# The second norm's scale and bias moved from the weights to ScalarE's copy out of PSUM

## The reference, cut to what matters

```python
def layer_norm(x, w, b, eps=1e-05):
    mu = jnp.mean(x, axis=-1, keepdims=True)
    var = jnp.mean(jnp.square(x - mu), axis=-1, keepdims=True)
    return (x - mu) * lax.rsqrt(var + eps) * w + b
...
# a feed-forward layer: attention on layer_norm(x, ln1_w, ln1_b) is added, then
def moe_ff(x, w_gate, w1, b1, w2, b2):       # x is layer_norm(., ln2_w, ln2_b)
    probs = jax.nn.softmax(t @ w_gate, axis=-1)
    tw, ti = lax.top_k(probs, TOP_K)          # 2 of 8 experts
    tw = tw / jnp.sum(tw, axis=-1, keepdims=True)
    for e in range(N_EXPERTS):
        we = jnp.sum(jnp.where(ti == e, tw, 0.0), axis=-1)
        h = jax.nn.gelu(t @ w1[e] + b1[e]) @ w2[e] + b2[e]
        out = out + we[:, None] * h
```

## Time and profile before

| | us |
|---|---|
| median of 3 runs | 1042.02 (1041.05 to 1045.36) |
| profiled execution | 1043.29 |
| its span, from the first to the last instruction | 1041.3 |
| busy TensorE / VectorE / ScalarE / GpSimd | 991.2 / 558.0 / 604.9 / 395.4 |
| mean granted TensorE clock | 0.959 of full speed |

### The profile page before, as it was taken

The page is one execution under the profiler, slowest core; times in us unless marked ns, Lnnn a source line. Parts: engine busy times, 40 slices in busy tenths (PEclk is TensorE's granted clock), DMA queues, the critical chain, the costliest instruction groups (busy, mean ns, idle before and its releaser), DMA issues.

```text
span 1041.3 us, 22226 instructions
## 1 busy us (share of the span) xinstructions
PE 991.2 (95%) x8516; PEld 745.7 (72%) x8516; DVE 558.0 (54%) x1427; ACT 604.9 (58%) x1128; POOL 395.4 (38%) x839
## 2 busy tenths in 40 slices
PE   3999999999999999999999999899999999999998
PEld 2655555666655999999886555566665699999997
DVE  4877777788884212122336788678888322111111
ACT  1356666887887454444445777688777744444443
POOL 6858676757743100012022353736873310000000
PEclk9677888999999999999999999899999999999999
DMA  8000000000000000000000000000000000000000
GB/s 286 2 2 2 3 2 2 3 3 3 3 3 2 1 1 1 2 1 1 1 2 1 3 3 2 3 3 3 3 2 3 2 2 4 8 1 11 1 11 11
DMA packets 9960, 10.42 MB, mean 10 GB/s; under 512 B 1528, under 2 KB 7552, under 8 KB 9856
## 3 DMA queue, kind: packets, MB, share of 16 engines
q1 hardware_dynamic: 8848, 7.64, 2.3%
q10 hardware_dynamic: 1008, 1.38, 0.4%
HBM read 7.44 MB, written 1.05 MB: 8 GB/s over the span
## 4 chain that ended last, share of the span: by engine, by line
PE 79%; DVE 15%; POOL 3%; issue 3%; ACT 0%; DMA 0%; DVEq 0%; ACTq 0%; POOLq 0%
PE bankR L625 22%; PE bankO L387 11%; PE bankE L406 8%; DVE M L986 7%; PE bankE L360 6%; PE bankE L614 6%; PE bankE L616 6%; PE bankE L615 6%; PE bankE L397 2%; DVE QKV L948 2%; PE bankR L373 2%; PE bankR L457 1%; PE bankR L427 1%; PE bankR L475 1%; PE bankE L467 1%
## 5 line engine op out<-in xcount | busy, mean ns | idle before, releaser
L986 DVE TENSOR_REDUCE M<-bankR 128x2 f32<-128x512 f32 x512 | 326.6, 684 | 97.2 <-PE bankR L373 95.9
L741 ACT ACTIVATE Pr<-bankE 128x512 f32<-128x512 f32 x512 | 277.5, 595 | 132.7 <-PE bankE L360 128.9
L845 ACT ACTIVATE Pr<-bankE,b1c 128x512 f32<-128x512 f32 x256 | 171.8, 689 | 176.1 <-PE bankE L616 175.0
L1141 DVE SCALAR_TENSOR_TENSOR X<-bankR,WE,X 128x128 f32<-128x128 f32 x256 | 72.1, 344 | 332.7 <-PE bankR L625 332.7
L625 PEld LDWEIGHTS bankR<-w,Pr 128*128 128x128 f32 x2048 | 238.3, 192 | 6.3 <-issue 1.1
L625 PE MATMUL bankR<-w,Pr 128*128 128x128 f32 x2048 | 238.8, 275 | 0.9 <-DVE X L1141 0.9
L373 PE MATMUL bankR<-KQ 32*128 32x256 f32 x1024 | 170.1, 346 | 6.6 <-DVE M L986 4.5
L387 PE MATMUL bankO<-Pr,Vx 128*32 128x256 f32 x2048 | 173.0, 413 | 0.6 <-ACT OT L733 0.5
L360 PEld LDWEIGHTS bankE<-KQ 32*128 32x128 f32 x1024 | 81.8, 194 | 101.5 <-issue 64.3
L360 PE MATMUL bankE<-KQ 32*128 32x256 f32 x1024 | 136.1, 343 | 0.0
L373 PEld LDWEIGHTS bankR<-KQ 32*128 32x128 f32 x1024 | 108.8, 197 | 16.2 <-DVE M L986 11.7
(11 more groups left out here) (166 smaller groups left out, 1185.7 us busy)
## 6 DMA issues: line engine op xcount, KB each, us to landing
THL<-in_w SPq DMA_DIRECT2D x1, 2048.0 KB, 8.9
KQ<-MT SPq DMA_DIRECT2D x128, 4.0 KB
X<-in_x SPq DMA_DIRECT2D x8, 128.0 KB, 6.6
out_x<-X SPq DMA_DIRECT2D x4, 256.0 KB, 2.3
ropeA<-in_ropeA ACTq DMA_DIRECT2D x1, 384.0 KB, 5.2
ropeB<-in_ropeB ACTq DMA_DIRECT2D x1, 384.0 KB, 5.5
w_lo_rope<-in_w_qkv_rope ACTq DMA_DIRECT2D x1, 192.0 KB, 2.9
b_qkv_rope<-in_b_qkv_rope ACTq DMA_DIRECT2D x1, 192.0 KB, 4.3
```

Of the source, the lines that this page charges most:

```text
L741: nc.scalar.activation(Pr[:, (h // HG) % 2, h % HG], act_bank("S", layer, b, h).rearrange("p (k q) -> p k q", k=TT), ACT.Exp, scale=EXP_SC ...
L845: nc.scalar.activation(G[:, e % 2, c, :], act_bank("hid", ph, at, c), ACT.Gelu_apprx_tanh, bias=b1c[:, e * FC + c:e * FC + c + 1]).then_in ...
L986: v.tensor_reduce(M[:, b % 2, :, h], dve_bank("raw", layer, b, h).rearrange("p (t k) -> p t k", t=TT), AX.X, ALU.max, negate=True).then_in ...
L1141: v.scalar_tensor_tensor(xt[:, j, t, :], dve_bank("out", ph, at)[:, t * D:t * D + D], WE[:, j * BT + t, e:e + 1], xt[:, j, t, :], ALU.mult ...
```

## The change

The second norm's scale and bias are laid on u itself. GpSimd's `close` leaves u in fp32 and does not split it. TensorE turns it by two fp32 transposes into half a bank. ScalarE's `do_uT` is two instructions: one activation (Identity) with the scale and the bias as columns of `lncols`, PSUM to the new tile UT in fp32, and a copy that rounds UT to THL's first half. VectorE's new `rest_of_u` takes the rest to THL's second half. The folding of scale and bias into w1, b1 and w_gate is gone on all engines; the one for b_qkv, which belongs to the first norm, stays in step m = (0, 0). TensorE's gate matmuls stand behind raw scores 5 in place of raw scores 4. VectorE's gate copy and `choose` stand behind maxima 5, `weigh` stands at the end of the step, and ScalarE's exponential for the gate behind its last exponentials. `early` also holds in the step in which p is block (3, 0). Tables of counts (`NFOLD`, `u_ready`, `uT_copied`) and the unused tiles follow.

The core of the diff:

```diff
             def do_uT(layer, b):
                 if LAYERS[layer] == "ffn":
-                    need(pe, u_ready, layer, b, 8)
+                    need(pe, u_ready, layer, b, 6)
                     ring_e.take(pe, ("uT", layer, b))
-                    for x in range(2):
-                        for t in range(TT):
-                            k = turn_r(act_bank("uT", layer, b), 2 * x + t, Uhl[:, x, t, :])
+                    for t in range(TT):
+                        k = turn(act_bank("uT", layer, b)[:, t * P:t * P + P], U[:, t, :], ident[:])
                     k.then_inc(uT.sem, 1)
-                    ring_e.give(("uT", layer, b), uT_copied, layer, b)
+                    ring_e.give(("uT", layer, b), uT_copied, layer, b, 1)
 
             def do_gate(layer, b):
                 if LAYERS[layer] == "ffn":
-                    need(pe, uT_copied, layer, b)
+                    need(pe, u_rest, layer, b)
                     ring_r.take(pe, ("gate", layer, b))
...
                     ring_r.give(("gate", layer, b), gate_copied, layer, b)
 
-            def do_fold(e):
-
-
-                if e == 0:
-                    pe.wait_ge(in_ffn, 8 * 16)
-                    pe.wait_ge(ready_pool, 7)
-                ring_r.take(pe, ("fold", e))
-                bank = dve_bank("fold", e)
-                if e == 0:
-                    mm(bank[:, 0:3 * D], lnb1[:], w_qkv["ffn"][:], start=True, stop=True)
-                    mm(bank[:, 384:384 + E], lnb2[:], w_gate[:], start=True, stop=True)
-                for c in range(FC):
-                    k = mm(bank[:, 400 + c:401 + c], w1raw[:, e, c * P:c * P + P], lnb2[:, 0:1], start=True, stop=True)
-                k.then_inc(fold, 1)
-                ring_r.give(("fold", e), folded, 0, 0, NFOLD - E + e + 1)
+            def do_fold():
+
+                pe.wait_ge(in_ffn, 8 * 16)
+                pe.wait_ge(ready_pool, 6)
+                ring_r.take(pe, ("fold",))
+                mm(dve_bank("fold")[:, 0:3 * D], lnb1[:], w_qkv["ffn"][:], start=True, stop=True).then_inc(fold, 1)
+                ring_r.give(("fold",), folded, 0, 0)
 
...
                 if t:
                     do_outT(*t)
-                if m and m[0] == 0:
-                    do_fold(m[1])
+                if m == (0, 0):
+                    do_fold()
                 if a:
...
                 if m:
                     do_raw(*m, 4)
+                if n and LAYERS[n[0]] != "rope":
+                    do_kT(*n)
+                if a:
+                    do_pv(*a, 1, 1)
+
+                if m:
+                    do_mT(*m, 0)
+                if a:
+                    do_scores(*a, 6)
+                if m:
+                    do_raw(*m, 5)
                 if u:
                     do_gate(*u)
-                if n and LAYERS[n[0]] != "rope":
-                    do_kT(*n)
-                if a:
-                    do_pv(*a, 1, 1)
-
-                if m:
-                    do_mT(*m, 0)
-                if a:
-                    do_scores(*a, 6)
-                if m:
-                    do_raw(*m, 5)
                 if t:
...
             def hidden(ph, at):
                 j, e = divmod(at, E)
                 if e == 0:
-                    need(pe, uT_copied, 2 * ph + 1, 2 * j + 1)
+                    need(pe, u_rest, 2 * ph + 1, 2 * j + 1)
                 if (ph, at) == (0, 0):
...
             def do_uT(layer, b):
                 if LAYERS[layer] == "ffn":
                     need(act, uT, layer, b)
-                    copy(THL[:, :, b, :], act_bank("uT", layer, b).rearrange("p (x t) -> p x t", x=2)).then_inc(uT_copied.sem, 1)
+                    need(act, u_rest, layer, b, 0)
+                    if (layer, b) == (1, 0):
+                        act.wait_ge(in_ffn, 8 * 16)
+                    nc.scalar.activation(UT[:], act_bank("uT", layer, b)[:, 0:T], ACT.Identity, bias=lncols[:, 3:4],
+                                         scale=lncols[:, 2:3]).then_inc(uT_copied.sem, 1)
+                    need(act, uT_copied, layer, b, 1)
+                    copy(THL[:, 0, b, :], UT[:]).then_inc(uT_copied.sem, 1)
 
...
                 if a:
                     do_exp(*a, 7)
+                if block_of(u) is not None:
+                    do_gate_exp(*block_of(u))
                 if n and LAYERS[n[0]] == "rope":
...
             def do_gate(layer, b):
                 if LAYERS[layer] == "ffn":
                     need(dve, gate, layer, b)
-                    if layer == 1 and b == 0:
-                        need(dve, folded, 0, 0)
-                    tt(LG[:, b], dve_bank("gate", layer, b)[:, 0:TT * E].rearrange("p (t e) -> p t e", t=TT),
-                       gbias[:].unsqueeze(1).broadcast_to([P, TT, E]), ALU.add).then_inc(gate_copied.sem, 1)
-
-            def do_fold(e):
-                dve.wait_ge(fold, e + 1)
-                bank = dve_bank("fold", e)
-                if e == 0:
-                    tt(b_qkv["ffn"][:].rearrange("p c d -> p (c d)"), bank[:, 0:3 * D],
-                       b_qkv["ffn"][:].rearrange("p c d -> p (c d)"), ALU.add).then_inc(folded.sem, 1)
-                    v.tensor_copy(gbias[:], bank[:, 384:384 + E]).then_inc(folded.sem, 1)
-                own = b1c[:, e * FC:e * FC + FC]
-                tt(own, bank[:, 400:400 + FC], own, ALU.add).then_inc(folded.sem, 1)
+                    v.tensor_copy(LG[:, b], dve_bank("gate", layer, b)[:, 0:TT * E].rearrange(
+                        "p (t e) -> p t e", t=TT)).then_inc(gate_copied.sem, 1)
+
+            def rest_of_u(layer, b):
+
+                if LAYERS[layer] == "ffn":
+                    need(dve, uT_copied, layer, b)
+                    tt(THL[:, 1, b, :], UT[:], as32(THL[:, 0, b, :]), ALU.subtract).then_inc(u_rest.sem, 1)
+
+            def do_fold():
+                dve.wait_ge(fold, 1)
+                tt(b_qkv["ffn"][:].rearrange("p c d -> p (c d)"), dve_bank("fold")[:, 0:3 * D],
+                   b_qkv["ffn"][:].rearrange("p c d -> p (c d)"), ALU.add).then_inc(folded.sem, 1)
 
...
                 if t:
                     divide(*t)
-                if m and m[0] == 0:
-                    do_fold(m[1])
+                if m == (0, 0):
+                    do_fold()
                 if m:
                     do_max(*m, 3)
                 if m:
                     do_max(*m, 4)
+                if u:
+                    rest_of_u(*u)
+                if nxt:
+                    norm_in(*nxt)
+                if m:
+                    do_max(*m, 5)
                 if u:
                     do_gate(*u)
                 if block_of(u) is not None:
                     choose(*block_of(u))
-                if nxt:
-                    norm_in(*nxt)
-                if m:
-                    do_max(*m, 5)
-                if block_of(u) is not None:
-                    weigh(*block_of(u))
                 if m:
                     do_max(*m, 6)
                 if t:
                     residual(*t)
                     norm3_in(*t)
+                if block_of(u) is not None:
+                    weigh(*block_of(u))
 
...
             def drain(ph, e):
                 layer = 2 * ph + 1
+                if e == 0:
+                    rest_of_u(layer, NB - 2)
                 if e == 1:
                     do_gate(layer, NB - 2)
                 if e == 2:
                     residual(layer, NB - 1)
                     norm3_in(layer, NB - 1)
+                if e == 4:
+                    rest_of_u(layer, NB - 1)
                 if e == 5:
...
                     need(pool, ln3_stats, layer, b)
                     moments(ev, layer, b, meanvar3[:, b % 2], lnsmall3, 0)
+                    need(pool, uT, layer, b, 0)
                     normalise(ev, U, Hs[:, b], lnsmall3)
-                    need(pool, ev, layer, b, 6)
-                    need(pool, uT, layer, b, 0)
-                    g.tensor_copy(Uhl[:, 0], U[:]).then_inc(ev.sem, 1)
-                    need(pool, ev, layer, b, 7)
-                    g.tensor_tensor(Uhl[:, 1], U[:], as32(Uhl[:, 0]), ALU.subtract).then_inc(ev.sem, 1)
                     g.tensor_tensor(X[:, b], X[:, b], Hs[:, b], ALU.add).then_inc(ev.sem, 1)
 
             def split_w1(e):
                 if e == 0:
                     pool.wait_ge(in_ffn, 8 * 16)
-                g.tensor_scalar(w1s[:, e, :], w1raw[:, e, :], lncols[:, 2:3], 1.0, ALU.mult, ALU.mult).then_inc(w1_scaled, 1)
-                pool.wait_ge(w1_scaled, e + 1)
-                g.tensor_copy(w1h[:, e, :], w1s[:, e, :]).then_inc(w1_split, 1)
+                g.tensor_copy(w1h[:, e, :], w1raw[:, e, :]).then_inc(w1_split, 1)
                 pool.wait_ge(w1_split, 2 * e + 1)
-                g.tensor_tensor(w1l[:, e, :], w1s[:, e, :], as32(w1h[:, e, :]), ALU.subtract).then_inc(w1_split, 1)
+                g.tensor_tensor(w1l[:, e, :], w1raw[:, e, :], as32(w1h[:, e, :]), ALU.subtract).then_inc(w1_split, 1)
 
             def prepare_ffn():
```

(6 more changed lines are left out.)

35 lines of the change are left out of this document (15 added, 20 removed).

## The result

The changed kernel takes 1032.2 us (median of six runs, 1029.73 to 1034.31) against 1041.79 (six runs). The ratio is 0.9907, 95% interval 0.9885 to 0.9928: 9.7 us less (7.5 to 12.0), where 15.9 were forecast. The profiled execution took 1029.73 us, the fastest of the six, against 1043.29 before, so its steps add up to 13.6 us; about 4 of these are chance in how often the clock fell. Two steps that the change does not touch, from 561 to 597 us before, hold 2.2 us of that: each had 3.4 us at half clock before and none after (17.41 and 18.24 us against 16.60 and 16.84).

What follows compares the result with a forecast made beforehand. No engine was taken as full in the rotary steps, TensorE as the bound in the mixtures. -1.8 - 10.2 - 1.0 - 5.2 + 3.6 - 1.3 = -15.9 us gave 1026 us, range 1011 to 1037.

Steps and rivals of the forecast that it cites:

- the likeliest case: Whole kernel: a time of 1019 to 1034 us, given a chance of 0.55.
- signs of being wrong: Rotary steps of 21 us or under 18, half clock from 225 us on, or a new wait at the gate.
- Step (0, 0): First rotary step: without the gate's and expert 0's folding and with earlier keys, 1.8 us less (bounds 1.0 and 2.5).
- The folds: Steps (0, 1) to (0, 6): 1.7 us less each, 10.2 in all (4.8 to 18); step (0, 7): 1.0 less.
- it ends where it ended: Rotary steps: if the half-clock stretch keeps its end, TensorE's lead is worth 0.8 to 1.2 us a step.
- it ends sooner: Rotary steps: if the half-clock stretch ends earlier, as TensorE no longer waits inside it, up to 3.0 us a step.
- the half clock goes: Rival, rotary steps: about 18.0 us each, 3.0 and not 1.7 less, total 1018 or 1010; chance 0.2 (below 1019).
- The handover: Layer 2 to layer 3: norm of block (3, 0) moves into GpSimd's idle stretch, 5.2 us less (2.7 to 6.1).
- Nothing else stopped TensorE there: Layer 2 to layer 3: with the 2.74 us wait the half-clock stretch goes too, giving back up to 3.4 us.
- The u steps: Steps with a block u: even ones 0, those with u = 1 and 3 +0.9 each, +3.6 us (0 to 5.2).
- The mixtures: Mixtures, bound by TensorE: four turns of u at 0.33 give 1.3 us less (bounds 0.5 and 1.4).
- The slower rival: Rival, u steps: TensorE's stops at the weighing bring half-clock stretches of 3.4 us each; eight give 1053; chance 0.08.

Runs made afterwards that it cites:

- The kernel with the norm in two: The changed kernel with GpSimd's norm of block (3, 0) cut in two, its rounding, subtraction and sum with the bias behind the keys; ratio 0.9863.
- The fastest kernel: The changed kernel with the norm of block (3, 0) cut in two and experts' weighing one step later; 1023.6 us, ratio 0.9800.

## Why the prediction was right, step by step

The time lies inside the stated range and in the likeliest case's own (1019 to 1034); the sum was 6 us too large. With what the runs and profiles show in place of its terms it is 0 - 6.3 - 0.9 - 4.2 (the middle of 3.4 and 5.0) + 2.6 - 0.9, so -9.7; that this is the measured figure to the tenth is chance, as single terms are uncertain by 2 us and more. The prediction's own signs of being wrong did in part appear: three of the six rotary steps lie outside its 18 to 21 us (two at 17.8, one at 22.0), and half clock stands at 295 and at 783 us. So the forecast was right where the gain comes from, and not in what the clock does.

**1. Step (0, 0), -1.8 forecast: wrong.** It won nothing. The 0.6 us more of the profile are no cost either: with this step as before, two other kernels took 19.37 and 19.38 us (the handover edit alone, one matmul per fold). The keys did come 2 us earlier on GpSimd, and the fold's eight passes are gone, but neither was what the step waited for. VectorE works without a gap from 29.2 to 40 us, so what TensorE gained it lost waiting for VectorE's addition to the fold's bank. VectorE, then TensorE:

```profile
33.66 0.96 DVE L966 TENSOR_TENSOR R<-QKV,ropeA 128x256 f32<-128x256 f32 x1
34.55 0.82 DVE L967 TENSOR_TENSOR R<-QKV,ropeB 128x256 f32<-128x256 f32 x1
35.30 0.54 DVE L1020 TENSOR_TENSOR b_qkv_ffn<-bankR,b_qkv_ffn 128x384 f32<-128x384 f32 x1
...
35.90 1.39 PE L370 MATMUL bankR<-KQ 32*128 32x256 f32 x4 [1.31 <-DVE b_qkv_ffn L1020]
```

Both kernels' matmuls run at half speed here, whatever the clock row says: the page after has no half clock recorded in this step, yet eight turns of the keys take 1.97 us in it, as before, and 1.12 at full clock. The kernel with the norm in two has the same step recorded at half clock from 32.2 us on, and it takes the same 19.42 us.

**2. The folds, -10.2 and -1.0: the mechanism right, the size not.** Step (0, 7) gave 0.9. For the six steps the folds' removal is worth 7.2 us in the runs less that 0.9, so 6.3, some 1.05 a step where 1.7 was taken. As forecast, the product follows the turn at once, and the wait ahead of maxima 3 is gone. The term that failed is the one between "it ends where it ended" and "it ends sooner". From 17.81 us at full clock, two kernels' sums without folds (117.31 with 32.7 us at half clock, the 2 us that the record misses put in, and 120.27 with 42.7) give 0.32 and 0.31 us lost per us at half clock. By that estimate, of the 11.4 us between the profiles 7.6 are clock (about 24 us less of it) and some 4 are the folds' own time. One profile has two steps at 17.8 us and another one, and runs of one kernel spread by 4 us and more; the clock's share in that spread is an inference from the profiles. The rival "the half clock goes" was half right: it went from some steps, wholly.

**3. The handover, -5.2: right in size by the runs (3.4 and 5.0), wrong in what follows.** The wait went. "Nothing else stopped TensorE there" failed: the moved norm collided with VectorE's R, and half clock came all the same. With the collision removed the step took 16.85 us, the 16.84 of its neighbour in the earlier trace rows, which is the 5.2 us of the forecast. The term held one thing too many at nothing: what the norm meets on VectorE in its new place.

**4. The u steps, +3.6: the sum about right (2.6 for the exchange of places alone), the place wrong.** Counted by TensorE's projections, the steps with u = 0 and u = 2 gained 0.15 us each rather than nothing, and those with u = 1 gained 0.1 rather than losing 0.9, as VectorE had room. What costs is the stop of 1.15 us in those with u = 3 and the half clock behind it: with u = 4 and 5 they took 1.5 us more in the first phase and 3.7 in the second, by the windows above. The prices of VectorE's and ScalarE's instructions were right, as the groups of the changed kernel show (0.57 and 0.42 us for ScalarE, 0.99 against 0.95 forecast; 0.43 for the subtraction). The two transposes take 0.44 us a block (7.0 us for 16) and not 0.3:

```profile
L775 ACT ACTIVATE UT<-bankE,lncols 128x256 f32<-128x256 f32 x16 | 9.1, 569 | 12.4 <-PE bankE L482 12.4
...
L482 PE MATMUL bankE<-ident,U 128*128 128x128 f32 x32 | 7.0, 303 | 0.0
L1016 DVE TENSOR_TENSOR THL<-UT,THL 128x256 fp32r<-128x256 f32 x16 | 6.8, 426 | 4.8 <-ACT THL L721 4.3
L721 ACT ACTIVATE THL<-UT 128x256 fp32r<-128x256 f32 x16 | 6.7, 417 | 0.5
```

**5. The mixtures, -1.3: there, with 0.9.** From the first to the last matmul of the experts, before, then after:

```profile
330.77:548.39 217.62, 217.46 (x1499) 197.03 (x1496) 54.53 (x191) 98.92 (x150) 26.11 (x61) 1.00 0.00 1
823.53:1029.89 206.36, 206.36 (x1421) 187.80 (x1419) 40.32 (x155) 92.83 (x139) 7.85 (x17) 1.00 0.02 5
```
```profile
319.78:536.95 217.17, 217.01 (x1495) 196.54 (x1493) 55.66 (x195) 98.98 (x152) 23.68 (x57) 1.00 0.00 1
810.62:1016.50 205.88, 205.88 (x1416) 187.29 (x1414) 41.48 (x159) 93.38 (x141) 5.42 (x13) 1.00 0.02 5
```

0.45 and 0.48 us for two blocks each, so 0.23 a block where 0.33 was taken; the price of the transposes accounts for it (0.68 less 0.44).

**The slower rival** had the right mechanism, half clock in the u steps behind a stop by the weighing, and far too many of them: two places, about 5 us in the profile, and the gain was not used up. A stop is not needed for it either: with the folds out 3.4 us at half clock stand at 262 us, in a step with u = 1 in which TensorE had no stop over 0.2 us (19.14 us against 17.71). Its other support fell. The fastest kernel has the same fp32 transposes of u, and its u steps and mixtures are at 1.00 throughout. The Trainium skill (TensorE: Matmul & The Clock Gate, Part 4: PE-mode transpose) does not count a transpose as activity; no run here shows an effect of that on the clock.

Open stays what exactly decides in a rotary step whether the clock falls: of six steps two escaped it in two kernels without folds, one in four others, none in any kernel with folds or with w1 behind the keys.

## What to carry to other kernels

A stop of TensorE of 1.15 to 1.35 us in a full step cost 2 to 4 us here where half clock (1.2 and not 2.4 GHz) followed, and 0.4 us in the one place where it did not. So look for such stops first. Then look for one-column matmuls: the profile counts them as busy, and behind them the half clock lasted longer than behind the same matmuls with 128 columns. Before moving GpSimd's work into its idle time, look at what VectorE does there; before moving VectorE's, ask who needs the result, and put it where that is, not where the last one stood.

## What the runs showed of the hardware that was not expected

- Eight fp32 passes over 128 columns take 1.16 us at full clock where eight over one column take 1.05, and the kernel with the wide ones is 9.2 us faster (0.9912), with 25.9 us at half clock in the rotary steps against 56.6.
- GpSimd and VectorE lengthen each other by whole instructions: R 0.68 to 1.16 us, the sum with the bias 0.73 to 1.18, a rotation product 0.41 to 1.48.
- The same stop of 1.14 to 1.15 us was followed by no half clock (a loss of 0.4 us) or by 3.4, 6.8 or 10.2 us of it; 10.2 us of it go with a loss of 4.4 us (44.21 against 39.83).
- The granted clock row can be at 1.00 while matmuls run at half speed, at the start of the program (1.97 us for eight turns); the durations tell, not the row.
